# Dispatch of a soft mixture of experts kept token-major, with the per-slot maxima and sums found by short transposes

## The reference

```
x = layernorm(x, norm_g, norm_b)
logits   = einsum('bnd,esd->bnes', x, se)                  # 512 tokens x 1024 slots
dispatch = softmax(logits, axis=1)                         # over the tokens, one slot at a time
combine  = softmax(logits.reshape(b, n, -1), axis=-1)      # over the slots, one token at a time
slots    = einsum('bnd,bnes->besd', x, dispatch)
gate, up, expert output from slots; result = einsum('bns,bso->bno', combine, eout)
```

## Time and profile before

| | before |
|---|---|
| median of three runs | 1235.87 us |
| lowest, highest | 1233.32, 1236.91 us |
| the profiled execution's own time | 1233.49 us |
| its span (first to last instruction) | 1231.8 us |
| mean granted TensorE clock | 0.983 |
| busy: PE, DVE, ACT, POOL | 96%, 63%, 55%, 36% |

### The profile page before, as it was taken

How to read it: one execution, slowest core, us unless ns; L and a number is a source line. 1 busy time by engine, 2 the same in 40 slices (tenths; PEclk the granted TensorE clock), 3 DMA queues, 4 the chain that set the end, 5 groups by cost and what they waited for, 6 DMA issues and landing times.

```text
span 1231.8 us, 19727 instructions
## 1 busy us (share of the span) xinstructions
PE 1183.5 (96%) x7126; PEld 932.5 (76%) x7126; DVE 780.0 (63%) x1330; ACT 673.2 (55%) x1042; POOL 448.2 (36%) x336
## 2 busy tenths in 40 slices
...
GB/s 144 142 113 113 138 95 128 126 132 126 138 129 148 91 163 83 207 62 36 89 123 114 120 121 180 103 120 245 157 162 167 171 179 179 111 210 132 233 248 54
DMA packets 126672, 170.32 MB, mean 138 GB/s; under 512 B 47041, under 2 KB 77186, under 8 KB 126594
## 3 DMA queue, kind: packets, MB, share of 16 engines
...
...
## 4 chain that ended last, share of the span: by engine, by line
PE 84%; DVE 7%; ACT 5%; DMA 1%; issue 1%; POOL 1%; SPq 1%; ACTq 0%; DVEq 0%; POOLq 0%
PE ring L414 11%; PE ring L416 10%; PE ring L415 10%; PE ring L1367 7%; PE ring L1511 7%; PE ring L1352 6%; PE tail L1378 6%; PE tail L414 3%; PE tail L416 3%; PE tail L415 3%; PE tail L1338 2%; PE ring L1354 2%; PE ring L1400 2%; PE tail L1511 2%; ACT x L825 2%; PE ring L1436 2%
## 5 line engine op out<-in xcount | busy, mean ns | idle before, releaser
L1079 DVE TENSOR_REDUCE mx<-ring 128x4 f32<-128x512 f32 (+2 forms) x192 | 200.5, 1046 | 88.7 <-PE ring L1354 88.2
L806 ACT ACTIVATE pt<-ring 128x1024 f32<-128x1024 f32 (+1 forms) x192 | 168.9, 881 | 100.3 <-PE ring L1367 76.0
L684 POOL TENSOR_SCALAR_AFFINE_SELECT pt<-pt 128x512 f32<-128x512 f32 x128 | 84.8, 663 | 194.4 <-ACT pt L806 193.9
L1352 PE MATMUL ring<-qks 96*128 96x384 f32 (+3 forms) x512 | 141.5, 365 | 7.7 <-DMA qks<-stg 3.6
L1367 PE MATMUL ring<-qks 98*128 98x256 f32 (+3 forms) x512 | 138.0, 373 | 8.6 <-DVE mx L1079 4.7
L1367 PEld LDWEIGHTS ring<-qks 98*128 98x128 f32 x512 | 78.6, 192 | 75.1 <-issue 38.7
L709 POOL TENSOR_TENSOR hl<-hid,hh 128x512 fp32r<-128x512 f32 x64 | 82.6, 1301 | 78.3 <-ACT hh L901 78.3
L1352 PEld LDWEIGHTS ring<-qks 96*128 96x128 f32 x512 | 92.0, 198 | 15.2 <-issue 5.1
L1188 DVE SCALAR_TENSOR_TENSOR hid<-ring,bias_e,gate 128x512 f32<-128x512 f32 x64 | 47.8, 748 | 80.9 <-ACT gate L895 47.2
L1378 PE MATMUL tail<-pt,va 128*32 128x512 f32 (+3 forms) x1024 | 95.9, 447 | 2.1 <-POOL pt L684 2.1
L1354 PE MATMUL ring<-maskb,identb 128*128 128x128 bf16 (+2 forms) x352 | 91.4, 260 | 0.0
...
## 6 DMA issues: line engine op xcount, KB each, us to landing
qks<-stg SPq DMA_DIRECT2D x384, 128.0 KB, 2.4
...
```

The costliest lines, as they stand in the source:

```text
L684: nc.gpsimd.affine_select(out=m, in_=m, compare_op=ALU.is_ge, fill=0.0, base=0, pattern=[[0, GH], [1, P]], channel_multiplier=-1).then_inc ...
L806: nc.scalar.activation(pt[j % 2][:, h:h + heads, 0:n], heads_of(tile, heads, n), ACT.Exp, scale=SCALE).then_inc(empty, 1)
L1079: nc.vector.tensor_reduce(out=mx[:, g, h:h + heads, i], in_=heads_of(tile, heads, (i + 1) * P), axis=AX.X, op=ALU.max).then_inc(empty, 1)
L1352: nc.tensor.matmul(scores[:, h, :], qks[0:KS_ROWS, g, 0, h0 + h, i * P:(i + 1) * P], qks[0:KS_ROWS, g, 1, h0 + h, 0:n], start=(h == k), st ...
```

## The change

Dispatch stays token-major throughout. The running maximum over the four 128-token tiles is kept in `xn` while `s1` comes in (DVE, an elementwise maximum for each tile after the first). One step `topT` of 8 transposes turns that 128 x 1024 array, and DVE reduces it to 8 negative maxima per partition, `m2`. One step `topB` of 8 transposes reads each column of `m2` with stride zero, 128 times over, which puts the maxima back as a 128 x 1024 tile that is the same in all partitions. DVE adds that tile to the logits (`sub`, four pieces), ACT makes the exponentials twice (`e`: once rounded to the high half `dh`, once in full into `e2`), POOL makes the low half (`lo`). The sums go the same way: POOL adds the four pieces of a half (`sum`), `sumT` (4 transposes) turns them, DVE reduces and inverts, `sumB` (4 stride-zero transposes) puts the inverses back, ACT copies them to SBUF, and DVE multiplies the slots by them as they leave PSUM. `s2`, `d` and `e2` are gone. The order tables and joins are written anew, and POOL has a table too.

```diff
-PE_FRONT = (("zT", 1), ("c2", 0, 0), ("c2", 0, 1), ("s2", 0, 0), ("s2", 0, 1), ("s2", 0, 2), ("slots", -1, 1), ("d", 0, 0),
+PE_FRONT = (
+    ("sumT", -1, 1), ("topT", 0), ("c2", 0, 0), ("zT", 1), ("sumB", -1, 1), ("topB", 0), ("slots", -1, 1), ("s1", 1, 0), ("c2", 0, 1),
+    ("c2", 0, 2), ("s1", 1, 1), ("sumT", 0, 0), ("s1", 1, 2), ("s1", 1, 3), ("sumB", 0, 0), ("slots", 0, 0), ("c2", 0, 3),
+)
...
+POOL_FRONT = (
+    ("lo", 0, 0), ("lo", 0, 1), ("sum", 0, 0), ("lo", 0, 2), ("lo", 0, 3), ("zl", 1), ("sum", 0, 1),
+)
...
-PE_JOIN = (55, 28, 28, 23, 23, 18, 18, 18, 17, 17, 14, 12, 12, 12, 5, 3, 3, 1, 1)
+PE_JOIN = (12, 6, 3, 2, 1)
...
+                    nc.gpsimd.tensor_tensor(out=dl[h][:, rows, :], in0=e2[u][:, :, :], in1=fp(dh[h][:, rows, :]), op=ALU.subtract).then_inc(d_low, 1)
+                    nc.gpsimd.tensor_tensor(out=e2[2 * h][:, :, :], in0=e2[2 * h][:, :, :], in1=e2[2 * h + 1][:, :, :], op=ALU.add).then_inc(summed, 1)
+                    pool.wait_ge(summed, n - 1)
+                    nc.gpsimd.tensor_tensor(out=e2[2 * h][:, 0, :], in0=e2[2 * h][:, 0, :], in1=e2[2 * h][:, 1, :], op=ALU.add).then_inc(summed, 1)
...
+                    nc.scalar.activation(dh[h][:, rows, :], e2[u][:, :, :], ACT.Exp)
+                    nc.scalar.activation(e2[u][:, :, :], e2[u][:, :, :], ACT.Exp).then_inc(e_made, 1)
+                    nc.scalar.activation(sls[h][:, 1, :], tile[:, 0, :], ACT.Copy).then_inc(empty, 1)
...
+                        nc.vector.tensor_tensor(out=most, in0=s1s[b % 2][:, 0, :] if n == 1 else most, in1=tile[:, :, :].rearrange("p k s -> p (k s)"),
+                                                op=ALU.max).then_inc(topped, 1)
...
+                    nc.vector.tensor_tensor(out=e2[u][:, :, :], in0=s1s[b % 2][:, rows, h * 512:(h + 1) * 512],
+                                            in1=bcast(pairs[slot(src)][:, h, :].unsqueeze(1), [P, 2, 512]),
+                                            op=ALU.add).then_inc(shifted if u < 3 else pair_drained[slot(src)], 1)
...
+                    blink(nc.vector.tensor_reduce(out=es[:, n], in_=tile[:, 0, :].rearrange("p (j q) -> p j q", q=P), axis=AX.X, op=ALU.add))
+                    nc.vector.reciprocal(res[:, n], es[:, n]).then_inc(empty, 1)
...
                     for d in range(NC):
-                        last = nc.vector.tensor_scalar(out=sls[h][:, d, :], in0=tile[:, d, :], scalar1=ng[:, d:d + 1], scalar2=nb_[:, d:d + 1],
-                                                       op0=ALU.mult, op1=ALU.add)
+                        last = nc.vector.scalar_tensor_tensor(out=sls[h][:, d, :], in0=tile[:, d, :], scalar=ng[:, d:d + 1], in1=sls[h][:, 1, :],
+                                                              op0=ALU.mult, op1=ALU.mult)
+                    blink(last)
+                    for d in range(NC):
+                        last = nc.vector.tensor_scalar(out=sls[h][:, d, :], in0=sls[h][:, d, :], scalar1=nb_[:, d:d + 1], scalar2=None, op0=ALU.add)
                     last.then_inc(empty, 1)
...
+                    for n in range(NS):
+                        last = nc.tensor.transpose(tile[:, n // 4, n % 4 * P:(n % 4 + 1) * P], bcast(m2[:, n:n + 1], [P, P]), ident[:, :])
+                    for j in range(4):
+                        last = nc.tensor.transpose(tile[:, 0, j * P:(j + 1) * P], bcast(res[:, 4 * h + j:4 * h + j + 1], [P, P]), ident[:, :])
```

More of the change, by code:

```diff
@@ new lines @@
+ACT_FRONT = (
+    ("c2", 0, 0), ("sumB", -1, 1), ("xn", 1), ("e", 0, 0), ("e", 0, 1), ("e", 0, 2), ("zh", 1), ("c2", 0, 1), ("s1", 1, 0), ("e", 0, 3),
+    ("c2", 0, 2), ("s1", 1, 1), ("s1", 1, 2), ("s1", 1, 3), ("sumB", 0, 0), ("c2", 0, 3),
+)
+DVE_FRONT = (
+    ("sumT", -1, 1), ("topT", 0), ("zT", 1), ("sub", 0, 0), ("sub", 0, 1), ("xn", 1), ("sub", 0, 2), ("sub", 0, 3), ("slots", -1, 1),
+    ("s1", 1, 0), ("s1", 1, 1), ("sumT", 0, 0), ("s1", 1, 2), ("s1", 1, 3), ("rows", 1), ("slots", 0, 0),
+)
@@ new lines @@
+POOL_FRONT = (
+    ("lo", 0, 0), ("lo", 0, 1), ("sum", 0, 0), ("lo", 0, 2), ("lo", 0, 3), ("zl", 1), ("sum", 0, 1),
+)
+SP_FRONT = (("c2", 0, 0), ("c2", 0, 1), ("slots", -1, 1), ("z", 2), ("slots", 0, 0), ("c2", 0, 2), ("c2", 0, 3))
+PE_LAST = (
+    ("topT", 0), ("c2", 0, 0), ("topB", 0), ("sumT", -1, 1), ("slots", -1, 1), ("sumB", -1, 1), ("c2", 0, 1), ("slots", 0, 0),
+    ("sumT", 0, 0), ("sumB", 0, 0), ("slots", 0, 1), ("sumT", 0, 1), ("c2", 0, 2), ("sumB", 0, 1), ("c2", 0, 3),
+)
+ACT_LAST = (
+    ("weight", 0, 3), ("weight", 0, 1), ("c2", 0, 0), ("e", 0, 0), ("e", 0, 1), ("e", 0, 2), ("c2", 0, 1), ("sumB", -1, 1),
+    ("weight", 0, 2), ("e", 0, 3), ("sumB", 0, 0), ("c2", 0, 2), ("sumB", 0, 1), ("weight", 0, 0), ("c2", 0, 3),
+)
@@ L113 @@
+DVE_LAST = (
+    ("topT", 0), ("sub", 0, 0), ("sub", 0, 1), ("sumT", -1, 1), ("sub", 0, 2), ("sub", 0, 3), ("weight", 0, 3), ("slots", -1, 1),
+    ("sumT", 0, 0), ("slots", 0, 0), ("sumT", 0, 1), ("slots", 0, 1), ("weight", 0, 1), ("weight", 0, 0),
+)
+POOL_LAST = (
+    ("lo", 0, 0), ("lo", 0, 1), ("sum", 0, 0), ("lo", 0, 2), ("lo", 0, 3), ("sum", 0, 1),
+)
 SP_LAST = (("weight", 0, 1), ("weight", 0, 2), ("weight", 0, 3), ("slots", -1, 1), ("slots", 0, 0), ("weight", 0, 0), ("weight", 1, 0),
@@ L122 @@
+ACT_JOIN = (7, 2, 2, 2, 1, 1, 1, 1, 1, 1, 1, 1, 1, 1, 1, 1, 1, 1, 1, 1, 1)
+DVE_JOIN = (4, 4, 4, 2, 2, 2, 1, 1, 1, 1, 1, 1, 1, 1, 1)
+SP_JOIN = (2, 1, 1, 1, 1, 1, 1, 1)
+POOL_JOIN = ()
+PAIR_STEPS = ("lat", "max", "exp", "v", "yTT", "cproj", "wv", "seT", "zT", "s1", "topT", "topB", "sumT", "sumB", "c2", "slots")
 MISC_STEPS = ("wqk", "neg", "yT")
@@ L213, in block_kernel @@
     cs = place("cs", [P, 2, NT], f32)
-    m2 = place("m2", [P, NT, 2], f32)
-    es = place("es", [P, NT, 2], f32)
-    res = place("res", [P, NT, 2], f32)
+    m2 = place("m2", [P, NS], f32)
+    es = place("es", [P, NS], f32)
+    res = place("res", [P, NS], f32)
     at[0] = temp_at
@@ L852, in _ @@
                         act.wait_ge(y_filled, B * G)
+                    elif b >= 2 and n == 0:
+                        read = ("topB", b - 2)
+                        act.wait_ge(pair_drained[slot(read)], fill_count(read))
                     nc.scalar.activation(s1s[b % 2][:, n, :].rearrange("p (k s) -> p k s", k=2), tile[:, :, :], ACT.Copy)
@@ L888, in _ @@
                 elif name == "weight":
+                    if st == ("weight", 0, 1):
+                        read = ("topB", B - 2)
+                        act.wait_ge(pair_drained[slot(read)], fill_count(read))
                     split_high(0, b, st[2])
```

181 lines of the change are left out of this document (90 added, 91 removed).

## The result

The changed kernel is slower: 1260.7 us (median of 4 runs, 1255.11 to 1263.61) against 1234.8 us (4 runs, 1233.32 to 1236.91). The ratio is 1.0203, with an interval of 1.0158 to 1.0248. The profiled execution took 1263.61 us with a span of 1261.9, 30.1 us more than the 1231.8 of before.

The account below looks back on a forecast made before the run. The prediction took PE's instruction count to bound the middle of the front, but not its ends. Gains of 2 + 14 + 1 = 17 us from 1233.5 gave 1216.5, or 1219 by the median; it took 1218, range 1204 to 1240.

Parts of the forecast that it names:

- PE, in the middle: Middle rounds: net 32 fewer transposes at 0.109 us each, 3.5 us less PE work, a round of 29.6 us.
- rival 4: PE's broadcasts or transposes come out dear, 1.9 us a round back, nothing saved, 1233 us; chance 0.04.
- The other engines in a round, and waits: Middle rounds: DVE, ACT and POOL stay under 29.6 us by sums; with waits 31.0 us, 14 gained over six rounds.
- the stall: Middle rounds: two scalings wait 2.4 us for POOL against 1.3 slack, 1.1 lost; with 0.3 at `topB`, 1.4 us.
- Rival 3: Middle rounds: all five SBUF-to-SBUF passes of DVE wait for whole POOL passes, 1245 to 1255 us; chance 0.14.
- the fast passes that the prediction asked about: DVE's scalings from SBUF in fast mode: if free of POOL's lock, the sum would be 6.6 us better.
- The end of attention: From first logits to round 1: attention ends at about 575 us, round 1 starts at about 607, 2 us gained.
- rival 2: At the ends, attention without overlap ends only 10 us earlier, eating the gain, about 1234 us; chance 0.09.
- a thin start: First round: maxima, `topT`, `topB`, `sub` and `xnl` in a line ahead of the next `s1` cost about 4.5 us.
- two scalings: Second half of slots: DVE's last two SBUF-to-SBUF passes each wait half a POOL pass, 1.2 us, 2.4 in all.
- The last round: Last round up to the experts' first matmul: 33.7 us by the chain of slots against 34.7 before, 1 us gained.
- The sum: Whole kernel: gains of 2 at attention's end, 14 in six rounds and 1 in the last, 17 us.

Follow-up runs that it names:

- e5: The changed kernel without DVE's additions of norm_b to the slots, the tile released after the products; 1239.5 us, ratio 1.0036 to the kernel before.
- e12: The changed kernel with DVE's products of slots left in PSUM and the norm_b additions reading them there; 1246.0 us, ratio 1.0091 to the kernel before.
- e14: e8 with joins as long as in the kernel before, on SP's loads of z too; 1233.8 us, ratio 0.9988 to the kernel before.
- e11: The changed kernel with DVE's layer norm of sequence 7 moved to the end of round 0; 1244.0 us, ratio 1.0095 to the kernel before.
- e2: The changed kernel with ACT's and DVE's first expert-weight splits moved behind the last exponentials; 1243.4 us, ratio 1.0059 to the kernel before.
- e8: The changed kernel with e2's and e11's edits and the norm_b additions made by ACT instead of DVE; 1220.6 us, ratio 0.9889 to the kernel before.
- e15: e8 run again beside the kernel before on the same chip; 1221.3 us, ratio 0.9889.

## Why the prediction was wrong

The span came out 47 us over the forecast (1261.9 against 1231.8 - 17 = 1214.8): 21 of them lie ahead of round 1 (6.7 up to attention's last projection, 14 behind it), 7.5 in the six rounds, 16.5 in the last one, 2 behind it.

**PE, in the middle: right.** Three groups of transposes after, 610 to 872 us, the stride-zero ones (`m`, `res`) beside those of `c`:

```profile
L1508 PE MATMUL tail<-ident,c 128*128 128x128 f32 x56 | 7.4, 274 | 0.5 <-DVE sls L1232 0.5
L1485 PE MATMUL ring<-ident,m 128*128 128x128 f32 x40 | 5.2, 273 | 1.0 <-DVE m L1198 1.0
...
L1498 PE MATMUL tail<-ident,res 128*128 128x128 f32 x12 | 1.8, 272 | 0.0
```

They take the same 272 to 274 ns. Four of `res` lie 0.44 us ahead of the next transposes (664.17 to 664.61), so 0.109 each, as for those of `z` (0.87 for eight), and eight of `m` lie 0.79 ahead of a 512-column matmul, as `s1s` did before; rival 4 falls. Without the additions (e5) rounds 2 to 5 took 29.75 to 29.79 us, against the 29.6 of the sum.

**The other engines in a round, and waits: the mechanism right, the size low.** The stretch of the two additions beside POOL, DVE and POOL after (timeline), answers to the earlier trace rows:

```profile
671.48 1.40 DVE L1228 SCALAR_TENSOR_TENSOR sls<-ring,ng,sls 128x512 f32<-128x512 f32 x2
672.92 3.82 DVE L1232 TENSOR_SCALAR sls<-sls,nb__52 128x512 f32<-128x512 f32 x2
...
682.83 0.18 DVE L1218 RECIPROCAL res<-es 128x4 f32<-128x4 f32 x1
...
673.92 2.53 POOL L721 TENSOR_TENSOR e<-e,e 128x1024 f32<-128x1024 f32 x1
...
681.99 2.41 POOL L716 TENSOR_TENSOR dl<-e,dh 128x1024 fp32r<-128x1024 f32 x1 [1.77 <-ACT e L908]
```

Two passes in the second half of slots were held, as in the forecast, by 2.9 us together and not 2.4; those of the first half and `xnl` were not, as POOL was idle. The mis-sized term is the stall. PE's idle times in a middle round are 1.19 + 0.27 + 0.24 = 1.7 us, but they count from the end of a record, which is longer than the matmul's share. From start to start the wait for the additions costs 1.4 us (2.22 from 674.57 to 676.79, where 0.79 is the distance without a wait), and those at `sumT` and behind `topT` cost 0.4 each: 2.3 us instead of the 1.4 taken, on PE's own 29.9 us, 32.2 in all. The first of the six rounds took 33.1: there PE also waited 1.12 us, at 633.65, for a drain by ACT, whose pass of the layer norm (4.03 us, from 628.66) stood in front. e12 shows that the hold's own price is at least 1.4 us a round, 8.5 over six. Rival 3, in which all five passes are held and rounds last longer than before, did not come. The Trainium skill, SBUF — State Buffer, section "Who interferes with whom", lets a DVE instruction with at most one SBUF input, outside the 2-port modes, go free. The trace agrees: products with one operand in PSUM (1.40 for two), the reciprocal (0.18) and e12's additions weren't held. The held additions have one SBUF input too, but are the fast passes that the prediction asked about: 0.44 us each where nothing holds them, against 0.71 from PSUM.

**The end of attention: its first half right, the first round wrong.** The last projection was forecast at 575 us. It came at 581.7 in this profile, and `topT` follows the projection by 3.5 us: in the other kernels with this attention the projection stood at 570 to 578, and before the change at 597.6. So attention ended 16 us earlier here and 19 to 28 elsewhere, not the 10 that rival 2 supposes. Rival 2 (attention alone gives the gain back) is refuted by that, and by e14, where mixing costs 12 us. The step that failed is the one from `topT` to round 1: I took 28.5 us (32 if the 575 is read as the projection's end) and it took 42.8. I counted the waits of a thin start (4.5 us; 4.24 measured, at 593.61) and ACT's pass of the layer norm, but not DVE's chain of tiny instructions, which the shorter join had moved behind the start of POOL's passes. Before, POOL had nothing to do there, and the chain was 4.3 us long. By the same rule I had weighed for two scalings, it was the worst victim in the kernel. In these rows a hold costs the rest of a POOL pass whatever the length of what is held, and here four in a row paid it in full. e11 gives 11.4 us back.

**The last round: wrong.** I walked the chain of slots (33.7 us) and left the weights out of it, at no cost. `ACT_LAST` set two of them ahead of the first exponential. SP issued them 4.5 to 7.1 us behind the round's start (825.98 to 828.58), no later than before (4.6 to 7.2), and the one that ACT's list takes first was issued last and was there 13.7 us into the round, while the exponentials could have begun at 5.3. Before, they didn't stand behind it. e2 gives 12.8 us back; two pairs of additions were still held there (3.70 and 4.11 us), and without that e8 has 33.2 and e15 34.3, around the 33.7 of the walk.

**The sum.** With the two places mended and the hold avoided (e8), the kernel stands at 1220.6 us, near the forecast of 1218, but only in another order of steps and in part by luck. Its span is 13.1 us under the one before: 0 ahead of round 1 (forecast 2), 14.3 in the six rounds (14), 1.5 in the last (1), less 2.7 behind it (0). The 14 agree by coincidence, since the forecast had 1.1 us of hold in each round and e8 has none. The changed tables did what the forecast took to be free, and that was worth 11.4 + 12.8 us. What stays open: 2.9 us of round 0, and 2 us in the first expert, where the granted clock was 0.86 over the first 16 us instead of 1.00.
